# A masked maximum on VectorE and a cut on GpSimd in place of triangle matmuls, with seven score banks dealt anew

## What is computed

```python
# layer 0: 16 heads of 8 features, sequences of 512; feed-forward with inputs and weights rounded to fp4 in blocks of 16
q = _GRID[jnp.searchsorted(_MID, jnp.abs(xb / scale))] * jnp.sign(xb / scale) * scale
# layer 1: causal attention with an alibi slope for each of 16 heads; then a ternary feed-forward
_tlin(x, w, s) = jnp.einsum('bsi,oi->bso', x, w) * s     # w1, w2: 128 -> 512; h1, h2: 512 -> 512; w3: 512 -> 128
# layer 2: full attention, 16 heads; then a receptance and key mix
# layer 3: a state-space block; then eight experts with a router
```

## Time and profile before

| | |
|---|---|
| median of 3 runs | 2267.12 us (2256.22 to 2276.95) |
| the profiled execution | 2266.32 us, span 2264.4 |
| mean granted TensorE clock | 0.927 |
| busy: TensorE | 1922.8 us (85%) |
| VectorE | 1326.2 us (59%) |
| ScalarE | 1113.8 us (49%) |
| GpSimd | 657.0 us (29%) |

### The profile page before, as it was taken

One profiled execution on the slowest core, in us unless ns is written; L12 is line 12 of the kernel. 1 busy time (PEld: TensorE's weight loads), 2 busy tenths in 40 slices (PEclk: granted clock), 3 DMA queues, 4 the chain that ended last, 5 costly groups with the idle time before them and its releaser, 6 DMA issues.

```text
span 2264.4 us, 34478 instructions
## 1 busy us (share of the span) xinstructions
PE 1922.8 (85%) x12909; PEld 797.5 (35%) x12909; DVE 1326.2 (59%) x2538; ACT 1113.8 (49%) x1741; POOL 657.0 (29%) x780
## 2 busy tenths in 40 slices
PE   2477787778778889999999999999999976899998
PEld 0122233233334443343443433323332324444443
DVE  1545656675657464544444656565588935677663
ACT  0144555545554444444444445556677874445432
POOL 2234444543444131211212112121122205444320
PEclk9787888888878899999999999999999987999999
DMA  7321122202321122022021120211222210000000
GB/s 185 70 57 39 19 57 57 57 15 42 62 62 25 34 57 57 15 43 57 1 57 40 20 57 15 43 36 22 57 57 57 57 45 3 1 5 10 5 5 14
DMA packets 70269, 91.58 MB, mean 40 GB/s; under 512 B 13228, under 2 KB 63772, under 8 KB 65228
## 3 DMA queue, kind: packets, MB, share of 16 engines
q1 hardware_dynamic: 64536, 84.42, 18.0%
q10 hardware_dynamic: 5568, 4.96, 0.9%
HBM read 49.10 MB, written 39.85 MB: 39 GB/s over the span
## 4 chain that ended last, share of the span: by engine, by line
PE 55%; ACT 6%; DVE 4%; issue 4%; DMA 1%; SPq 1%; POOL 1%; DVEq 0%; POOLq 0%; ACTq 0%
PE ps L255 8%; PE ps L1156 6%; PE ps L1134 5%; PE ps L223 4%; PE ps L2869 3%; PE ps L171 2%; PE ps L2154 2%; PE ps L2156 2%; PE ps L2172 2%; PE ps L239 2%; PE ps L196 2%; DVE mx L415 2%; PE ps L1114 2%; ACT Pr L334 1%; ACT Pr L326 1%
## 5 line engine op out<-in xcount | busy, mean ns | idle before, releaser
L415 DVE TENSOR_REDUCE mx<-ps 128x2 f32<-128x1024 f32 (+3 forms) x512 | 408.5, 819 | 416.9 <-PE ps L202 205.5
L326 ACT ACTIVATE Pr<-ps 128x1024 f32<-128x1024 f32 (+3 forms) x512 | 359.6, 702 | 436.2 <-PE ps L177 303.8
L255 PE MATMUL ps<-Pr,V 128*32 128x256 f32 (+3 forms) x4096 | 382.8, 448 | 5.7 <-ACT ctxU L340 4.6
L426 DVE TENSOR_REDUCE mx<-ps 128x1 f32<-128x512 f32 x512 | 320.8, 681 | 96.9 <-PE ps L239 96.0
L334 ACT ACTIVATE Pr<-ps 128x512 f32<-128x512 f32 x512 | 282.5, 598 | 152.7 <-PE ps L223 148.9
L171 PE MATMUL ps<-Qst,Kst 64*128 64x512 bf16 (+3 forms) x1024 | 174.2, 337 | 109.2 <-ACT Pr L326 106.5
L196 PE MATMUL ps<-Kst,Qst 63*128 63x512 bf16 (+3 forms) x1024 | 160.0, 336 | 118.4 <-DVE mx L415 102.8
L223 PE MATMUL ps<-Qst,Kst 64*128 64x512 bf16 x512 | 166.5, 386 | 18.0 <-ACT Pr L334 7.2
L171 PEld LDWEIGHTS ps<-Qst,Kst 64*128 64x128 bf16 x1024 | 50.6, 95 | 287.8 <-ACT Pr L326 166.5
L239 PE MATMUL ps<-Kst,Qst 63*128 63x512 bf16 x512 | 144.4, 388 | 2.3 <-DVE mx L426 2.1
L1134 PE MATMUL ps<-f_shared,w_L_h1T 128*128 128x512 f32 x256 | 139.8, 638 | 0.0
(11 more groups left out here) (320 smaller groups left out, 3238.0 us busy)
## 6 DMA issues: line engine op xcount, KB each, us to landing
Qst<-parts_scratch SPq DMA_DIRECT2D x48, 384.0 KB, 5.5
Kst<-parts_scratch SPq DMA_DIRECT2D x48, 384.0 KB, 8.7
parts_scratch<-qpart SPq DMA_DIRECT2D x48, 192.0 KB, 2.7
parts_scratch<-kpart SPq DMA_DIRECT2D x48, 192.0 KB, 2.7
parts_scratch<-qpart SPq DMA_DIRECT2D x48, 128.0 KB, 2.7
parts_scratch<-kpart SPq DMA_DIRECT2D x48, 128.0 KB, 2.7
parts_scratch<-qpart SPq DMA_DIRECT2D x48, 64.0 KB, 2.3
parts_scratch<-kpart SPq DMA_DIRECT2D x48, 64.0 KB, 2.3
```

Source lines behind the costliest of these rows:

```text
L255: mm = pe.matmul(k.ps[32 * a:32 * a + 32, PV, lo:hi], k.V[:, b.par, jt, 4 * q + a, :], k.Pr[:, g % 2, a, lo - (T - W):hi - (T - W)], start ...
L326: act.activation(k.Pr[:, g % 2, 2 * tile:2 * tile + 2, 0:W], k.ps[:, PAIR_T:PAIR_T + 2, 0:W], ACT.Exp)\
L415: dve.tensor_reduce(heads[:, :, 4 * i + it:4 * i + it + 1], k.ps[:, PAIR_M:PAIR_M + 2, lo:lo + W], AX_X, ALU.max, negate=True).then_inc(se ...
L426: dve.tensor_reduce(k.mx[:, half, at:at + 1], k.ps[:, self.bank_m(n, u, hosting), :], AX_X, ALU.max, negate=True).then_inc(self.s_max.sem, 1)
```

## The change

- Banks: three for T (0 to 2), two for M (3 and 4), one for the guest (5). Context and misc keep theirs. Every layer now deals T to the three banks a head at a time, and a head's matmul waits for the exponential three heads before it.
- The triangle matmuls are gone. In the alibi layer the maximum of a head is one `tensor_tensor_reduce` on VectorE, which adds `tri_row` (a row mask of large negative numbers) and takes the maximum, and GpSimd's `affine_select` sets the exponentials above the diagonal to zero in `Pr`, one for each group of four heads. The context matmuls wait for that cut.
- Exponentials are taken for each head, four instructions in place of two. Maxima are taken for each head, too.
- The guest runs on one bank. A slot's guest is in two halves, behind the M scores of part 0 and at the end of part 3.
- The order within a slot on TensorE is T0, M0, first half of the guest; T1, context; M1 in odd slots, output product, second half, misc.
- The ternary Silu is moved from slot 3 to the end of slot 4, Gelu of the h2 product is at the end of slot 9, and Gelu of the h1 product at the end of slot 14; slot 15 has no guest units. The residual goes from the middle of slot 13 to its end, and the output product to part 3. Two fp4 steps move by a part.

```diff
-PAIR_T, PAIR_M, GUEST, PV, MISC = 0, 2, 4, 6, 7
+BANKS_T, BANKS_M, GUEST, PV, MISC = 0, 3, 5, 6, 7
...
+        if kind == "alibi":
+            self.s_cut = k.started("attention_cut", GROUPS)
...
+    def fills(self, c):
 
 
         pair, phase = divmod(c, 2)
-        return pair, (((6 + 8 * pair - 4, (0, 2)), (8 * pair + 6, (1,))) if phase else ((8 * pair, (3,)),))
+        u = 8 * pair
+        if phase:
+            return pair, ((0, (0, 2), u + 2, u + 1), (1, (0, 2), u + 4, u + 2),
+                          (0, (1,), u + 6, u + 4), (1, (1,), u + 7, u + 6))
+        return pair, ((0, (3,), u, u - 1), (1, (3,), u + 1, u))
...
+    def bank_t(self, b, g, j):
+        return BANKS_T + (64 * (b.c + NB * self.index) + 4 * g + j) % 3
...
-        pe.wait_ge(self.s_exp.sem, self.s_exp.at(b, 2 * g + tile))
+        pe.wait_ge(self.s_exp.sem, self.s_exp.at(b, 4 * g + 2 * tile - 1))
...
-        if tri:
-            for part in range(2):
-                for a in (1, 0):
-                    rows = slice(64 * a, 64 * a + 64)
-                    mm = pe.matmul(ps[:, PAIR_T + a, 0:P], k.ident_h[rows, part, :], k.tri_kq[rows, part, :],
-                                   start=False, stop=part == 1)
-        mm.then_inc(self.s_scores_t.sem, 1)
-
-    def pe_scores_m(self, pe, n, c, r):
+            pe.matmul(ps[:, self.bank_t(b, g, 2 * tile + 1 - a), 0:W], k.Kst[rows, b.par, 2 * q + tile, P * jt:P * jt + P],
+                      k.Qst[rows, b.par, 2 * q + tile, T - W:T], start=True, stop=True)\
+              .then_inc(self.s_scores_t.sem, 1)
...
+        for i in range(count):
+            for a, its, u, free in fills:
+                if i == 0 and u == 0:
+                    pe.wait_ge(self.s_stacked.sem, self.s_stacked.at(n))
+                if i == 0:
+                    pe.wait_ge(self.s_max.sem, self.s_max.at(n, free))
+                W, lo = self.span(its[i]), self.place(its, its[i])
+                rows, at = slice(64 * a, 64 * a + MROW), P * its[i]
+                mm = pe.matmul(ps[:, BANKS_M + a, lo:lo + W], k.Qst[rows, n.par, pair, at:at + P],
+                               k.Kst[rows, n.par, pair, 0:W], start=True, stop=True)
+                if i == count - 1:
+                    mm.then_inc(self.s_scores.sem, count)
...
-        earlier = 4 * g + j - (1 if hosting else 2)
-        pe.wait_ge(self.s_exp.sem, self.s_exp.at(b, earlier if b.c else max(earlier, 0)))
-        pe.matmul(k.ps[:, self.bank_t(b, g, j, hosting), :], k.Kst[rows, b.par, 2 * q + tile, P * jt:P * jt + P],
+        pe.wait_ge(self.s_exp.sem, self.s_exp.at(b, 4 * g + j - 2))
...
+            pe.wait_ge(self.s_exp.sem, self.s_exp.at(b, 4 * (g + 1)))
+            if self.kind == "alibi":
+                pe.wait_ge(self.s_cut.sem, self.s_cut.at(b, g + 1))
...
+        act.activation(k.Pr[:, g % 2, 2 * (j // 2) + 1 - j % 2, 0:W], k.ps[:, self.bank_t(b, g, j), 0:W], ACT.Exp)\
+           .then_inc(self.s_exp.sem, 1)
 
...
+        for a, its, u, _ in fills[2 * r:2 * r + 2]:
+            dve.wait_ge(self.s_scores.sem, self.s_scores.at(n, u + len(its)))
+            if u % 32 == 0:
+                dve.wait_ge(self.s_mT_ps.sem, self.s_mT_ps.at(n.plus(-1), half + 1))
+            for it in its:
+                W, lo = self.span(it), self.place(its, it)
+                at = 16 * a + 4 * i + it
+                scores = k.ps[:, BANKS_M + a, lo:lo + W]
+                if self.kind == "alibi":
+                    dve.tensor_tensor_reduce(scores, scores, k.tri_row[:, T - W:T], 1.0, -3e38, ALU.add, ALU.max,
+                                             k.mx[:, half, at:at + 1]).then_inc(self.s_max.sem, 1)
+                else:
+                    dve.tensor_reduce(k.mx[:, half, at:at + 1], scores, AX_X, ALU.max, negate=True)\
+                       .then_inc(self.s_max.sem, 1)
...
+    def pool_cut(self, pool, b, g, zero):
+
+        diagonal = self.k.Pr[:, g % 2, :, 0:P]
+        pool.wait_ge(self.s_exp.sem, self.s_exp.at(b, 4 * g + 4))
+        pool.affine_select(diagonal, diagonal, [[0, 4], [1, P]], ALU.is_ge, zero, base=0, channel_multiplier=-1)\
+            .then_inc(self.s_cut.sem, 1)
...
+        pe.wait_ge(self.s_raw.sem, self.s_raw.at(n, t))
+        pe.matmul(self.k.ps[:, GUEST, 0:self.HID], self.xT[:, P * t:P * t + P],
...
-            elif here == (10, 0):
+            elif here == (10, 1):
...
-            elif here == (13, 1):
+            elif here == (13, 0):
...
-    UNITS = ((("turn",), ("h2", 0, 0), ("h2", 0, 1)),
-             (("h2", 0, 2), ("h2", 0, 3), ("gate", 0)),
-             (("gate", 1), ("gate", 2), ("gate", 3)),
...
-             (("down", 1), ("down", 2), ("down", 3)),
...
+    HALVES = ((("turn",),), (("h2", 0, 0),),
+              (("h2", 0, 1), ("h2", 0, 2)), (("h2", 0, 3),),
+              (("gate", 0),), (("gate", 1),),
+              (("gate", 2),), (("gate", 3),),
+              (("h2", 1, 0), ("h2", 1, 1)), (("h2", 1, 2), ("h2", 1, 3)),
...
+              (), ())
     FIRST = 11
-    SILU, GELU_B, GELU_A = 3, 9, 14
+    SILU, GELU_B, GELU_A = 4, 9, 14
...
+        if at == 1:
+            return
+        for unit in self.HALVES[2 * s + at // 2]:
...
-        if at:
+        if not at:
...
     def pe_quarter(self, pe, F, s, part, b, g, pb, pg, mb, c):
-        hosting = F < self.LONE
         t, tn = self.of(b)
-        if t:
-            if t.kind == "full":
-                t.pe_head_t(pe, tn, g, part, hosting)
-            elif part % 2 == 0:
-                t.pe_scores_t(pe, tn, g, part // 2)
-        if part in (0, 2):
-            self.pe_guest(pe, F, s, part)
+        if t and t.kind == "full":
+            t.pe_head_t(pe, tn, g, part)
+        elif t and part % 2 == 0:
+            t.pe_pair_t(pe, tn, g, part // 2)
         m, mn = self.of(mb)
-        if m:
-            if m.kind == "full":
-                m.pe_head_m(pe, mn, c, part, hosting)
-            elif part % 2 == 0:
-                m.pe_scores_m(pe, mn, c, part // 2)
         p, pn = self.of(pb)
+        if p and p.kind != "full" and part == 2:
+            p.pe_context(pe, pn, pg, 0, 1)
+        if m and m.kind == "full":
+            m.pe_head_m(pe, mn, c, part, F < self.LONE)
+        elif m and part in (0, 3):
+            m.pe_round_m(pe, mn, c, part // 3)
         if p and p.kind == "full" and part % 2:
             p.pe_context(pe, pn, pg, part // 2, 2)
-        elif p and p.kind != "full" and part == 3:
-            p.pe_context(pe, pn, pg, 0, 1)
-        if part == 1:
-            self.pe_guest(pe, F, s, part)
+        if part == 0:
+            self.pe_guest(pe, F, s, 0)
+        elif part == 3:
             self.pe_out(pe, F, s)
+            self.pe_guest(pe, F, s, 2)
...
     def act_exps(self, act, F, s, b, g):
         t, tn = self.of(b)
-        if t and t.kind == "full":
-            for j in range(4):
-                t.act_head_exp(act, tn, g, j, F < self.LONE)
-                if j == 1:
-                    self.act_guest(act, F, s, 0)
-            return
-        if t:
-            t.act_exps(act, tn, g, 0)
-        self.act_guest(act, F, s, 0)
-        if t:
-            t.act_exps(act, tn, g, 1)
+        for j in range(4):
+            if t:
+                t.act_exp(act, tn, g, j)
+            if j == 1:
+                self.act_guest(act, F, s, 0)
...
-                self.dve_guest(dve, F, s, 0)
-                self.dve_maxima(dve, F, mb, c, 0)
-                self.dve_between(dve, F, s)
-                self.dve_guest(dve, F, s, 1)
+                for part in range(4):
+                    self.dve_maxima(dve, F, mb, c, part)
+                    if part == 0:
+                        self.dve_guest(dve, F, s, 0)
+                    elif part == 1:
+                        self.dve_between(dve, F, s)
+                        self.dve_guest(dve, F, s, 1)
                 self.dve_guest(dve, F, s, 2)
-                self.dve_maxima(dve, F, mb, c, 1)
                 self.dve_rest(dve, F, s)
...
-        if s == 13 and p and p.kind != "full":
-            p.dve_residual(dve, pn)
...
+        if s == 13 and p and p.kind != "full":
+            p.dve_residual(dve, pn)
...
+            for s, _, (pb, pg), _ in slots(F):
+                p, pn = self.of(pb)
+                if p and p.kind == "alibi":
+                    p.pool_cut(pool, pn, pg, zero)
...
+    c["tri_row"] = bf16_bits(np.where(j[None, :] - (T - P) > i[:P, None], NEG, 0.0))
```

237 lines of the change are left out of this document (76 added, 161 removed), and 20 rows, old and new, of tables (HALVES, UNITS).

## The result

The changed kernel takes 2253.43 us (median of ten runs, 2247.87 to 2257.55), the kernel before 2269.25 (ten runs): ratio 0.9936, interval 0.9917 to 0.9955. It is faster by 0.6%, where the prediction had it slower by 1.9%, at 2310. The profiled execution has a span of 2252.9 us, 11.5 less than that of before.

The account below looks back on a forecast made before the run. TensorE was taken to bound frames 12 to 15, a relay between engines the block frames. From 2266 us: +30 (frames 12 to 15), +3 (frame 11), +18 (16 to 18), -7 (block) gave 2310; range 2222 to 2362.

Parts of the forecast that it names:

- Block frames 1 to 7 ... Net -1, seven times -7: Block frames: third T bank -3.7, doubled maxima +1.3, residual +1.4; net -1 us each, -7 in all.
- The bank's term, -3.7: Block frames, slots 0 to 4: three T banks take about half of TensorE's 9.1 us wait for ScalarE.
- the +2.7 against it: Block frames: doubled maxima add 1.3 us in slots 4 to 8, and the later residual adds 1.4.
- three banks loosen the relay: Rival, chance 0.18: frames up to 10 gain up to 60 us, likelier 35; frames 12 to 15 gain 14; time 2217.
- Frames 12 to 15, +30 forecast: Alibi with ternary guest: idle 14.6 us in place of 3.4, triangles -7.0, clock +3.3; net +7.5 each.
- the guest bank: Frames 12 to 15: TensorE waits for VectorE to read the single guest bank, 4.0 us a frame; 1.4 in frames 16 to 18.
- The triangles: Alibi frames: dropping 64 groups at 0.11 us saves TensorE 7.0 us, counted in full in each of frames 12 to 15.
- the clock's term, 3.3: Frames 12 to 15: lower granted clock after the new pauses costs 3.3 us each; frames 16 to 18, 1.5 each.
- What VectorE, ScalarE and GpSimd got: Extra work per alibi frame: VectorE +15 us (bounds +5, +35), ScalarE 5.4, GpSimd 18; hidden in frames 12 to 15.
- Frame 11: Frame whose Gelu is already bare, with a 3.74 us TensorE wait behind it: +3 us.
- Frames 16 to 18: Full attention, ternary guest: Silu +1.9, Gelu +2.6, guest bank +1.4, clock +1.5, third bank -1.4; +6 us each, +18.
- Frames 8 to 10: Alibi with fp4 guest: triangles -7.0 and third bank against VectorE's +15 beside the quantizer, cut and residual; 0 us.

## Why the prediction was wrong

**The step that failed is "Block frames 1 to 7 ... Net -1, seven times -7"**, and with it the worth of the third T bank. Measured: -38.6 us in frames 0 to 7. The run with two T banks puts 29.2 of that down to the bank. Two errors.

- Frame 0 had no term at all, and frame 1 was priced like the later ones. The two went from 152.57 to 134.07 us: -18.5 where the sum had -1. They host no guest, VectorE has only some 8 us of quantizing in the two (the weights, once, and the start of the first tile), and the relay that the earlier trace rows showed was all there was to gain from. The bank gave 7.6 in each.
- Frames 2 to 7 went from 436.09 to 416.03 us: -3.3 a frame where the sum had -1. The bank's term, -3.7, was not too small there: it measures -2.3, or -3.1 against the trace of the version with the activations mid-slot, whose block frames run the same code. (That 29.2 over eight frames also makes 3.7 is chance.) What was wrong is the +2.7 against it, and what was left out. The residual did cost 1.4 a frame, as said, but the maxima in pairs gave nothing back for the 1.3 of the doubled maxima, and the new order in the slot and the per-head work, which had no term, are worth the rest, 2.4 a frame by this account. No run here tells those apart, and they are not far above the differences between traces of the same code.

The bank had no term in frames 11 to 15 either, where it is worth 6.0 and 6.7 us. With these the windows show 42 us for it, and the medians 46.5.

The rival "three banks loosen the relay" had this mechanism, and "-35 if VectorE takes over half" for the frames up to 10; they measure -37.6. That it comes so near is in part luck, since 29.2 of it is the bank's, all in frames 0 to 7, and none in 8 to 10. What it wrongly held was that frames 12 to 15 would keep half the triangles' gain. The range, 2222 to 2362, took 2253 in for the sake of the rivals; the forecast itself had the sign wrong.

**Frames 12 to 15, +30 forecast, +14.6 measured.** The places were right: Silu 3.31 us (3.1), Gelu 4.79 (4.5), residual 1.49 (1.5). Mis-sized: the guest bank 2.6 (4.0), and the cut's wait 0.3 (1.5; over the four frames 1.8 for 6.0). Idle time went to 12.9 a frame (14.6). The triangles, taken out of the kernel before, give 5.2 and not 7.0. TensorE's busy time fell by 6.0 a frame, more than the 3.7 that -7.0 and +3.3 of clock leave. Moving the activations takes 7.5 a frame off, 5.2 of idle and 2.3 of busy time; the clock's term, 3.3, was of the right kind and a microsecond too large, if all of the 2.3 is the clock.

**What VectorE, ScalarE and GpSimd got** was less than forecast. In frames 12 to 15 VectorE has 4.8 us more a frame (+15 forecast, and +5 as its lower end), since the second instruction of a masked maximum runs inside the next one; ScalarE has 1.9 (5.4), and GpSimd 9.9 (18), at 0.668 us for a cut and not 1.1. That this work is hidden in frames 12 to 15, as the sum had it, held.

**Frame 11**, +3 forecast, -3.7 measured: I had reasoned that its Gelu is bare already and left out the triangles, worth 3.8 there, and the third bank, worth 6.0. With two banks it is +2.4.

**Frames 16 to 18**, +18 forecast, +17.2 measured; mid-slot activations give 19.0 back, so that part of the mechanism is shown too (in frame 17 TensorE waits 2.37 us behind the Silu and 3.83 behind the Gelu). That the guest bank (+1.4) and the third T bank (-1.4) cancel in these frames was not tested.

**Frames 8 to 10**, 0 forecast, +1.0 measured, and that is luck: the triangles are worth -10.0 (I had left them at nothing, as TensorE has idle time), the masks cost 17.7, and the remaining -6.7 belong to parts that no run here tells apart. "Hidden except behind the next tile's layernorm on Pool: once a frame, 1.5 us" named the right place and the wrong size: 4.27, 4.62 and 3.31 us. The term saw the layernorm on GpSimd, but not that it waits for VectorE's statistics itself, which in these frames stand behind the quantizer's steps on VectorE.

**The clock.** It fell as forecast behind the new pauses, to 0.94 from 1.00 over frames 12 to 15. The page of the Trainium skill, "TensorE: Matmul & The Clock Gate", section "Part 1: The HAM clock gate (the "warmup" mystery)", says that activity releases the throttle. The rows of this kernel agree in so far as the clock was low behind both pauses of frame 13 (0.70 and 0.67) and 0.97 over frames 12 to 15 with both under other work; they don't show why one pause of 3.31 us left it at 1.00.

## What to carry to other kernels

In a relay between engines price a further buffer over every frame that is a relay, the plain ones first: here the frames without a guest gained 7.6 us each and those with one 2.3, and a limit seen in one row of one slot is not the limit of the frame. A long activation with its table loads belongs between two pieces of work that its neighbour has already been given; here its place within one slot was worth 52 us by the medians and 49 by the windows, three times the whole change. And before a small step is put on a mostly idle engine with another engine waiting for it, read in each kind of frame what stands ahead of it in that engine's queue, and what that in turn waits for.

## What the hardware showed unexpectedly

- An affine_select of 128x512 on GpSimd takes 0.668 us by the profile, less than its plain elementwise steps of that size (1.043 and 1.392).
- The second instruction of a masked maximum, 0.140 us, adds nothing that can be seen when another maximum follows: the next one starts with it, 0.61 us after the first (128x512).
- Of two pauses a frame, 4.79 and 3.31 us in frame 13 and 3.83 and 2.37 in frame 17, moving the longer under other work gave 15.6 us in frames 12 to 18 and the shorter then 33.5. TensorE's idle time fell by about 16 us each time, but its busy time only with the second, when the granted clock went from 0.94 to 0.97 and from 0.97 to 1.00. Moving the Silu alone was not tried, so the order may have a part in it.
- The same pause of 3.31 us was followed by 9.30 us at a granted clock of 0.70 in one version and by 9.28 us at 1.00 in another.
- An edit that reduced TensorE's idle time by 20.6 us in frames 0 to 7 lengthened them by 13.4, as the same matmuls took 34 us more busy time. The clock's means, 0.80 for 0.83, account for about half of that.
